# A two-layer token MLP with group norms on one core: the fp16 copy of the first half of layer 2's GELU moves from ScalarE to GpSimd, and the hand-written orders change

## What is computed

```
x = x + hadamard(gn(x))                      # channels mixed by a 192x192 part of a 256 Hadamard matrix
x = x + conv(gn(x), W1, b1, g1, beta1, W2, b2, g2, beta2, W3, b3)

conv(x):                                     # per pixel, over the 192 channels
    h = gelu(layernorm(W1 x + b1) * g1 + beta1)     # layer 1, exact gelu
    h = gelu(layernorm(W2 h + b2) * g2 + beta2)     # layer 2
    return W3 h + b3                                # layer 3
```

## Time and profile before

| | us |
|---|---|
| median of 3 runs | 929.8 |
| lowest, highest | 927.72, 930.69 |
| the profiled execution | 930.58 |
| its span, first to last instruction | 928.8 |
| TensorE clock granted, mean over the span | 0.985 |

### The profile page before, as it was taken

How to read it: one execution, slowest core, us unless ns; L and a number is a source line. 1 busy time by engine, 2 the same in 40 slices (tenths; PEclk the granted TensorE clock), 3 DMA queues, 4 the chain that set the end, 5 groups by cost and what they waited for, 6 DMA issues and landing times.

```text
span 928.8 us, 22221 instructions
## 1 busy us (share of the span) xinstructions
PE 828.8 (89%) x8353; PEld 551.4 (59%) x8353; DVE 797.6 (86%) x1416; ACT 815.8 (88%) x2400; POOL 549.9 (59%) x414
## 2 busy tenths in 40 slices
PE   0546889899999999999999999999999999889897
PEld 0114556466666666666666666666666666566663
DVE  6798899899999999999999999999997888645455
ACT  0787879699998999999999999899999998999982
POOL 0453546467666566666765666666656666677760
PEclk9986999999999999999999999999999999999999
DMA  9825022224233233233242332333112113121213
GB/s 275 222 76 138 1 70 69 74 69 134 77 96 97 86 111 101 74 103 108 87 124 69 103 108 69 108 103 106 37 41 67 37 46 93 40 69 35 70 36 102
DMA packets 52090, 81.99 MB, mean 88 GB/s; under 512 B 14608, under 2 KB 14736, under 8 KB 51856
## 3 DMA queue, kind: packets, MB, share of 16 engines
q1 hardware_dynamic: 51984, 80.58, 28.8%
HBM read 41.23 MB, written 39.32 MB: 87 GB/s over the span
## 4 chain that ended last, share of the span: by engine, by line
PE 47%; DVE 33%; ACT 9%; POOL 5%; issue 2%; DMA 1%; SPq 1%; ACTq 0%; DVEq 0%; POOLq 0%
PE tm L571 12%; DVE z L1241 7%; PE tm L566 6%; DVE X L1082 5%; PE tp L583 5%; DVE xs_lo L1073 4%; DVE bn L1099 4%; POOL ge_lo L936 4%; PE hl L480 3%; PE hl L411 3%; ACT z L722 3%; PE tm L560 3%; DVE bn L1059 3%; DVE x_lo L1223 2%; PE tp L590 2%; PE hl L509 2%
## 5 line engine op out<-in xcount | busy, mean ns | idle before, releaser
L936 POOL TENSOR_TENSOR ge_lo<-ge,ge_hi 128x512 f16<-128x512 f32 (+1 forms) x190 | 311.6, 1650 | 152.0 <-ACT ge_hi L752 151.7
L928 POOL TENSOR_TENSOR rs<-ssq,neg_half 128x4 f32<-128x4 f32 x196 | 205.6, 1049 | 153.4 <-ACT z L722 151.5
L722 ACT ACTIVATE z<-tm 128x194 f32<-128x194 f32 x784 | 250.0, 337 | 37.2 <-PE tm L571 36.1
L1241 DVE TENSOR_TENSOR z<-tm,rs 128x768 f32<-128x768 f32 x196 | 186.0, 949 | 56.9 <-POOL rs L928 56.7
L734 ACT ACTIVATE ge<-tp,par 128x512 f32<-128x512 f32 x196 | 155.1, 791 | 17.2 <-PE tp L583 17.2
L722 ACT ACTIVATION_READ_ACCUMULATOR z<-tm 128x1 f32 x784 | 167.5, 214 | 0.0
L752 ACT ACTIVATE ge_hi<-ge 128x512 f16<-128x512 f32 (+1 forms) x190 | 161.0, 851 | 4.0
L1082 DVE SCALAR_TENSOR_TENSOR X<-hl,h_bias,X 128x512 f32<-128x512 f32 x138 | 98.7, 741 | 38.0 <-PE hl L416 37.7
L583 PE MATMUL tp<-cst,z 128*128 128x128 f32 x784 | 121.1, 277 | 5.8 <-ACT ge L734 5.6
L699 ACT ACTIVATE x_hi<-X,gscale 128x512 f16<-128x512 f32 x144 | 104.5, 736 | 14.1 <-DVE gshift L1179 14.1
L1223 DVE SCALAR_TENSOR_TENSOR x_lo<-X,gscale,x_hi 128x512 f16<-128x512 f32 x144 | 103.4, 743 | 3.0 <-ACT x_hi L699 2.4
(11 more groups left out here) (192 smaller groups left out, 1887.9 us busy)
## 6 DMA issues: line engine op xcount, KB each, us to landing
out<-X SPq DMA_DIRECT2D x48, 512.0 KB, 2.9
X<-x SPq DMA_DIRECT2D x40, 512.0 KB, 4.0
out<-X SPq DMA_DIRECT2D x98, 128.0 KB, 3.0
X<-x SPq DMA_DIRECT2D x80, 128.0 KB, 4.1
X<-x SPq DMA_DIRECT2D x8, 576.0 KB, 4.2
X<-x SPq DMA_DIRECT2D x16, 144.0 KB, 4.3
X<-weights SPq DMA_DIRECT2D x1, 1024.0 KB, 13.3
out<-X SPq DMA_DIRECT2D x8, 64.0 KB, 3.2
```

The source lines that it names most:

```text
L722: last = nc.scalar.activation(z[n][:, 2 * h + k, i * TW:(i + 1) * TW], tm[h][:, i, k * TW:(k + 1) * TW], ACT.Square, scale=float(C) ** -0. ...
L928: nc.gpsimd.tensor_tensor(rs[n][:, 2 * h:2 * h + 2, :], ssq[n][:, 2 * h:2 * h + 2, :], neg_half[0:TT, 0:4].rearrange("p (i k) -> p i k", i=2),
L936: nc.gpsimd.tensor_tensor(ge_lo[n][:, g % 2, PART[h], :], ge[n][:, PART[h], :], ge_hi[n][:, g % 2, PART[h], :], ALU.subtract).then_inc(s_g ...
L1241: nc.vector.tensor_tensor(z[n][:, 2 * h:2 * h + 2, 0:2 * C].rearrange("p k (i o) -> p i k o", i=2), tm[h][:, :, 0:2 * TW].rearrange("p i ( ...
```

## The change

`gelu_hi(g, 1, 0)`, ScalarE's fp16 copy of the first half of layer 2's GELU (128x512), is left out in every order; a new GpSimd function `gelu_copy(g)` writes the same copy, with a semaphore of its own. Beside this, the orders of `first` are rewritten on PE, ACT, POOL and DVE, and those of `step` on ACT, POOL and DVE. `last` and `drain` differ only by the copy.

```
+            def gelu_copy(g):
+
+                if not 0 <= g < NL or splits_on_dve(g, 1):
+                    return
+                pool.wait_ge(s_ge[1], 3 * g + 1)
+                if g >= 2:
+                    pool.wait_ge(s_l3, 2 * (g - 1))
+                nc.gpsimd.tensor_copy(ge_hi[1][:, g % 2, PART[0], :], ge[1][:, PART[0], :]).then_inc(s_ge_hi_pool, 1)
...
             def gelu_lo(g, n, h):
                 if not 0 <= g < NL or splits_on_dve(g, n):
                     return
-                pool.wait_ge(s_ge_hi[n], 2 * g + h + 1)
+                if (n, h) == (1, 0):
+                    pool.wait_ge(s_ge_hi_pool, g + 1)
+                else:
+                    pool.wait_ge(s_ge_hi[n], (2 * g + h if n == 0 else g) + 1)
...
             def gelu_hi(g, n, h):
-                if not 0 <= g < NL or splits_on_dve(g, n):
+                if not 0 <= g < NL or splits_on_dve(g, n) or (n, h) == (1, 0):
                     return
```

In `step`, POOL and ACT (ACT's first `scaled_hi` now stands ahead of the first squares; the second ahead of the next ones):

```
                 gelu_lo(g - 2, 1, 1)
+                rstd(g, 0, 1)
                 groupnorm_rstd(gn2_pair(g), 1)
-                rstd(g, 0, 1)
...
                 gelu_lo(g, 0, 1)
+                gelu_copy(g - 1)
                 gelu_lo(g - 1, 1, 0)
```

```
             def step(g):
+                scaled_hi(xs_unit(g, 0), 0)
                 squares(g, 0, 0, 0)
...
                 gelu_hi(g - 2, 1, 1)
-                scaled_hi(xs_unit(g, 0), 0)
+                scaled_hi(xs_unit(g, 0), 1)
                 squares(g, 0, 1, 0)
                 squares(g, 0, 1, 1)
-                scaled_hi(xs_unit(g, 0), 1)
...
                 gelu(g - 1, 1, 0)
-                gelu_hi(g - 1, 1, 0)
```

In `step`, DVE:

```
                 residual(h_unit(g, 0), 0)
                 residual(h_unit(g, 0), 1)
+                stats_x1(h_unit(g, 0), 0)
                 normalise(g, 0, 0)
-                stats_x1(h_unit(g, 0), 0)
                 residual(h_unit(g, 0), 2)
```

In `first`, one of many moves on DVE, and POOL's place for the copy:

```
                 stats_part(g, 5, 6)
+                residual(h_unit(g, 0), 0)
                 gn_stats(gn1_pair(g), 0)
-                residual(h_unit(g, 0), 0)
-                residual_left(h_unit(g, 0))
+                stats_x1(h_unit(g, 0), 0)
                 residual(h_unit(g, 0), 1)
```

More of the change, by code:

```diff
@@ L613, in first @@
                 h_ab(h_unit(g, 1))
+                h_c(h_unit(g, 1))
                 transposes(g - 1, 1, 0)
-                h_c(h_unit(g, 1))
                 h_left(h_unit(g, 1))
@@ L764, in first @@
                 scaled_hi(xs_unit(g, 0), 2)
+                split_left(g)
+                gelu(g, 0, 0)
+                split_x1(unit_at(g + 1), 0)
+                gelu_hi(g, 0, 0)
                 squares(g - 1, 1, 0, 0)
-                split_x1(unit_at(g + 1), 0)
+                squares(g - 1, 1, 0, 1)
                 split_x1(unit_at(g + 1), 1)
-                gelu(g, 0, 0)
-                squares(g - 1, 1, 0, 1)
                 split_x1(unit_at(g + 1), 2)
-                gelu_hi(g, 0, 0)
                 scaled_hi(xs_unit(g, 1), 0)
-                scaled_hi(xs_unit(g, 1), 1)
-                gelu(g, 0, 1)
                 squares(g - 1, 1, 1, 0)
                 squares(g - 1, 1, 1, 1)
+                gelu(g, 0, 1)
+                scaled_hi(xs_unit(g, 1), 1)
                 scaled_hi(xs_unit(g, 1), 2)
@@ L941, in first @@
                 rstd(g, 0, 1)
+                gelu_lo(g - 2, 1, 1)
                 groupnorm_rstd(gn2_pair(g), 1)
-                gelu_lo(g - 2, 1, 1)
+                rstd(g - 1, 1, 0)
                 groupnorm_rstd(gn1_pair(g), 0)
-                rstd(g - 1, 1, 0)
                 gelu_lo(g, 0, 0)
                 rstd(g - 1, 1, 1)
+                gelu_copy(g - 1)
                 gelu_lo(g, 0, 1)
@@ L1318, in first @@
                 scaled_lo(xs_unit(g, 1), 2)
+                normalise(g - 1, 1, 1)
                 residual(h_unit(g, 1), 0)
                 residual(h_unit(g, 1), 1)
-                normalise(g - 1, 1, 1)
-                residual(h_unit(g, 1), 2)
                 stats_x1(h_unit(g, 1), 0)
                 stats_x1(h_unit(g, 1), 1)
+                residual(h_unit(g, 1), 2)
                 residual_left(h_unit(g, 1))
@@ L1335, in step @@
                 residual(h_unit(g, 0), 1)
+                stats_x1(h_unit(g, 0), 0)
                 normalise(g, 0, 0)
-                stats_x1(h_unit(g, 0), 0)
                 residual(h_unit(g, 0), 2)
                 gn_var(gn2_pair(g), 1)
+                split_left_lo(g)
                 stats_x1(h_unit(g, 0), 1)
+                scaled_lo(xs_unit(g, 0), 0)
                 gn_var(gn1_pair(g), 0)
-                split_left_lo(g)
-                scaled_lo(xs_unit(g, 0), 0)
+                gn_shift(gn2_pair(g), 1)
+                scaled_lo(xs_unit(g, 0), 1)
+                scaled_lo(xs_unit(g, 0), 2)
                 residual_left(h_unit(g, 0))
-                scaled_lo(xs_unit(g, 0), 1)
-                gn_shift(gn2_pair(g), 1)
-                scaled_lo(xs_unit(g, 0), 2)
                 normalise(g, 0, 1)
```

40 lines of the change are left out of this document (18 added, 22 removed).

## The result

The changed kernel takes 949.1 us (median; 948.05 to 951.24), the kernel before beside it 930.3. The ratio is 1.021, 95% interval 1.0192 to 1.0228: 2.1% slower. The forecast was 937.3 us with a range to 943. The direction is right, the size is not: 19 us were lost where 7.5 were forecast.

What follows compares the result with a forecast made beforehand. TensorE was taken to bound plain steps, VectorE group-norm steps, and a loop of waits through GpSimd the last steps. Last steps +5.4, regular steps +4.8 and first six -2.7 gave +7.5 on 929.8: 937.3 us, range 927 to 943.

Steps and rivals of the forecast that it cites:

- The statistics ahead of z: Regular steps: one stats_x1 ahead of z makes TensorE idle 0.39 us in twelve plain steps; 4.7 us, +4.8 with steps 38, 39.
- The cast's own price: GpSimd's cast of 128x512, one per unit: estimated 0.85 us, between 0.64 and 1.16.
- c: Assumed cost of one GpSimd cast of 128x512, taken as 0.85 us.
- the seventh place: z of step 41, counted beside z of steps 43 to 48 as paying one cast; 0.54 us came off for step 42.
- each c is paid in full: Last steps: GpSimd's queue is the critical chain, so seven casts of 0.85 us, less 0.54, give +5.4 us.
- The cast costs nothing in the regular steps: Regular steps: GpSimd's queue has 1.1 us of room and the cast takes 0.85, so no cost there.
- The room ahead of z: Step 24: 1.1 us between the end of GpSimd's rs and the start of VectorE's z, said to absorb the cast.
- the costly rival: Cast blocks VectorE where it sets the pace, or costs as much as the subtraction; 941 to 950 us, chance 0.11.
- The dismissal of the rule: GpSimd blocking VectorE's two-SBUF-input instructions was set aside because 129 such instructions took only 731 to 816 ns.
- The first six steps: Steps 0 to 5: the new order wins a quarter of VectorE's 10.6 us idle time; -2.7 us, from 0 to -6.
- It costs nothing: First six steps: the cast can run while ScalarE still makes the copy gelu_lo(g, 0, 1) waits for; no cost.
- ScalarE's relief: ScalarE loses 25 to 30 us of work, worth at most 0.16 us in remainder-2 steps and 0.54 in step 42.

Runs made afterwards that it cites:

- a_filler: Changed kernel with eight filler matmuls of 512 columns ahead of layer 2's product in each of the six last steps; 941.2 us, ratio 1.0119.
- b_copy: Kernel before with the cast alone moved to GpSimd, directly ahead of gelu_lo(g-1,1,0) in all four orders; 950.1 us, ratio 1.0209.
- a_reduce: Changed kernel with five small VectorE group-norm instructions written as one-input sums over an axis of length 1; 945.1 us, ratio 1.0163.
- b_stats: Kernel before with only bn_stats moved ahead of the normalisation of layer 1's first half in regular steps; 934.4 us, ratio 1.0032.
- a_no_copy: Changed kernel with all its new orders, but the copy back on ScalarE at the end of its order; 937.7 us, ratio 1.0084.
- a_stt: Changed kernel with five small VectorE group-norm instructions written as scalar_tensor_tensor, same two SBUF inputs and values; 949.8 us.

## Why the prediction was wrong in size

**The statistics ahead of z: right.** Forecast 0.39 us of wait and plain steps of 16.28; measured 0.32 and 16.24, and 4.0 us for this edit alone against 4.8. That a matmul starts 0.14 us behind z, the slack and the direction held.

**The cast's own price: right in mechanism, too high.** c was taken as 0.85 us. The changed kernel's rows give

```profile
L936 POOL CAST ge_hi<-ge 128x512 f16<-128x512 f32 x47 | 28.9, 616 | 17.8 <-ACT ge L735 17.8
```

616 ns, with 0.07 of issue ahead of the subtraction, and 0.67 us in a step. That is at the lower end of the range, ScalarE's 641 ns, and at the 0.68 that the prediction worked out for a growing part that halves with one input, before it went above it. The 769 ns of the Trainium skill, "GPSIMD Engine Reference", section 3.1, are also above it. Steps 41 to 47 without the clock's part (a_filler) and the rest behind them give 3.4 + 0.7 = 4.1 us against +5.4. Steps 41 and 42, the seventh place, are worth -0.1 of it together.

**The missing step: what a longer wait does to the clock.** The term that failed most is "each c is paid in full", seven times c and nothing else in the last steps: +5.4 forecast, +10.3 measured from step 41 on. The prediction read the earlier trace rows, added c to the loop, and left TensorE's own speed as it was. The granted clock was 1.00 in these steps before, with a wait of 1.52 us in each. The wait of 2.18 us brought stretches of 3.4 us at 1.2 GHz, 1.6 us each. a_filler shows it by taking away the idle time and nothing else: -6.2 us. This is the largest single term of the result, it was in no rival, and without it the time, 941.2 us, would lie in the range.

**"The cast costs nothing in the regular steps": wrong, by two mechanisms.** The room ahead of z, 1.1 us, was read in step 24 alone, a step with remainder 0, and there it holds (15.89 in b_copy). There GpSimd's first subtraction starts 0.01 us behind the step's border. In step 25 of b_copy it starts 0.60 us behind it (517.40 against 516.80); rs ends at 522.29, z starts at 522.32, 5.52 us into the step instead of 5.35 (517.81 less 512.46). VectorE works without a pause from there to the second z, TensorE's fourth product starts 11.32 us into the step instead of 11.14, and remainder 1 takes 16.06. One step was read for all: in step 25 of the kernel before rs ended at 517.28, so the room was 0.53 us there, less than even the measured cast. The same late rs lengthens remainders 3 and 4 of b_copy, where z starts 0.16 to 0.17 us later and no group-norm instruction is held in remainder 3. In the group-norm steps VectorE sets the pace, as forecast, and GpSimd reached into it: the held instructions, 2.9 us by a_reduce. In the prediction this was the costly rival's condition, with 12.8 us for a hold of c in each of fifteen steps; the mechanism came true at a quarter of that price. A third, smaller one: the remainder-4 steps take 17.83 instead of 17.63 both in the changed kernel and in a_reduce, about 1 us in all. b_stats has 17.64 there and a_no_copy 17.93, so some other move of the new orders does this, without the cast too; `residual_left` moved behind all three `scaled_lo` there, but no run tests that move alone.

**The dismissal of the rule was the faulty inference.** The earlier trace rows show 129 two-input instructions of VectorE of 731 to 816 ns, and GpSimd busy 59%. From this the prediction concluded that nothing is held. But in that trace none of the 129 overlaps one of GpSimd's subtractions: none was exposed, so their lengths say nothing. A line that was exposed stood in the same trace:

```profile
L1158 DVE TENSOR_TENSOR gsq<-gmu x16: 161/163/1841, 28.4 to 787.0; 128x4 f32<-128x4 f32 x16
```

A maximum eleven times the median on a line of 4 elements is the sign to look for. That one starts 0.3 us into a GpSimd subtraction and ends 0.02 us behind it, in step 41, and stood on the critical chain. The traces bear the rule out, and the prediction had a rival with its price.

**The first six steps: wrong sign.** -2.7 forecast, +1.4 measured. a_no_copy gives +0.7 for the new order alone, b_copy +1.2 for the copy alone. VectorE's idle time was taken as a reserve of which a quarter could be had; steps 3 and 5 do get shorter, but the four others longer. "It costs nothing", said of the cast here, was wrong as well: the changed kernel takes 118.21 us and a_no_copy 117.52, so the cast costs 0.7. Part of the shift between steps is the clock: a stretch of 3.4 us at the lower level stands in step 2 now instead of in step 3. It goes with the order: all seven traces with the new first order have it in step 2, all seven with the old one in step 3. It moves time between the two steps; it isn't one stretch more. Steps 2 and 3 after; before, step 2 took 21.39 us at a clock of 1.00 and step 3 took 20.70 at 0.92:

```profile
106.81:130.33 23.52, 20.77 (x180) 12.44 (x179) 20.50 (x29) 16.56 (x50) 11.64 (x9) 0.93 0.11 36
130.33:149.62 19.29, 17.35 (x173) 11.47 (x173) 18.40 (x42) 16.65 (x50) 12.09 (x10) 1.00 0.13 41
```

**ScalarE's relief: right.** 22 us less work (25 to 30 forecast), and no stage got faster by it.

**What stays open.** The terms on the regular steps depend on the order in which they are added (the statistics 4.0 us before, 2.2 after; the copy 5.0 before, none on the new orders), so a split of the 7.1 us has no single answer. Why step 44 of the changed kernel keeps its clock isn't settled: TensorE waits 2.16 us for z there, 2.18 in step 45, and step 42 of b_copy fell with a wait of 1.97. In a_stt step 43 keeps it with a wait of 2.32 and step 44 loses it with 2.17. So the length of the one wait isn't the whole rule; that the added idle time brought the falls is what a_filler shows.

## What to carry to other kernels

When work is added to a loop of waits, add it to the idle time of TensorE too, and look what the granted clock did at waits of that length: here the clock cost nearly twice what the added instruction did (6.2 us against 3.4), and eight useless matmuls gave it back. Work that must go to the busy queue of such a loop belongs behind the instruction that the loop waits for; that place was worth some 15 us here with the copy and 3 without it. And a row can speak against contention only if its instructions ran beside the other engine: look for the exposed line, a short one with a maximum many times its median, before a rule is set aside.

## What the runs showed of the hardware

- The granted clock fell to half for 3.4 us at a time, in four of the five steps 43 to 47, with waits of TensorE of 2.16 to 2.33 us in all five, and in none of them in the kernel before, with 1.49 to 1.55 us. In b_copy it fell in step 42 with 1.97 us. One stretch cost about 1.6 us.
- A GpSimd subtraction or cast on a tile that was already running held VectorE's tensor_tensor, scalar_tensor_tensor and tensor_scalar on SBUF operands until 0.02 us behind its end, up to 1.84 us for an instruction of 161 ns. Beside GpSimd's 128x4 instructions for rs (1.0 us) the same VectorE lines took 161 to 165 ns. A reduction (157 ns), a tensor_tensor with one operand in PSUM (161 ns, largest 164), bn_aggr and bn_stats were not held.
- GpSimd's cast of 128x512 from fp32 to fp16 takes 616 ns in the mean, its two-input subtraction of the same tile 1166.
